# A decoder megakernel: one block end without GpSimd's drain, an earlier clearing of semaphores, and another order of the first norms of the causal attention

## The reference

```
x = x + linear_attention_and_small_experts(layernorm(x))     # layer 0
x = x + latent_cross_attention(ctx, layernorm(x))
x = x + shared_expert(n) + routed_experts(n)                 # n = layernorm(x), 8 experts, the best 2, capacity 640
x = x + causal_attention(layernorm(x))                       # layer 1, 16 heads of width 8
x = x + biased_causal_attention(layernorm(x), ctx)
x = x + best_expert(layernorm(x))
```

```
routed[token] = w0[token] * result[2 * token] + w1[token] * result[2 * token + 1]
```

## Time and profile before

| | |
|---|---|
| median of 3 runs | 1916.84 us (1915.33 to 1916.89) |
| the profiled execution's own time | 1922.22 us |
| its span, first to last instruction | 1920.4 us |
| TensorE busy | 94% of the span |
| VectorE, ScalarE, GpSimd busy | 65%, 46%, 33% |
| mean granted TensorE clock | 0.984 of full |
| routed experts end, causal attention starts | about 1260 to 1270 us into the span |

### The profile page before, as it was taken

How to read it: one execution, slowest core, us unless ns; L and a number is a source line. 1 busy time by engine, 2 the same in 40 slices (tenths; PEclk the granted TensorE clock), 3 DMA queues, 4 the chain that set the end, 5 groups by cost and what they waited for, 6 DMA issues and landing times. The chain is left out here.

```text
span 1920.4 us, 49670 instructions
## 1 busy us (share of the span) xinstructions
PE 1809.4 (94%) x19996; PEld 1346.2 (70%) x19996; DVE 1243.8 (65%) x2977; ACT 885.8 (46%) x1701; POOL 633.0 (33%) x748
## 2 busy tenths in 40 slices
PE   5899999999999999999999999978998999999978
PEld 2566666667888888888755667846766788888743
DVE  5666766646766666666643223237886888888876
ACT  1444444345555555555432213345673444545435
POOL 2111111113333333333314523333221444444547
PEclk8999999999999999999999999988999999999999
DMA  9200000000000000000010002210010000000001
GB/s 333 69 1 0 0 0 0 1 1 1 1 1 0 0 0 0 0 0 0 1 77 29 29 22 94 95 46 25 27 18 25 2 3 3 3 3 2 3 6 39
DMA packets 37909, 46.15 MB, mean 24 GB/s; under 512 B 4984, under 2 KB 32427, under 8 KB 37250
## 3 DMA queue, kind: packets, MB, share of 16 engines
q1 hardware_dynamic: 34434, 38.43, 6.3%
q0 software_dynamic: 3328, 5.58, 0.9%
HBM read 28.67 MB, written 17.10 MB: 24 GB/s over the span
## 5 line engine op out<-in xcount | busy, mean ns | idle before, releaser
L155 POOL TENSOR_TENSOR rstd<-var_eps,minus_half 128x2 f32<-128x2 f32 (+1 forms) x116 | 92.1, 794 | 477.8 <-DVE var_eps L149 477.5
L1052 POOL TENSOR_TENSOR xa_probs<-xa_probs,xa_total 128x512 f32<-128x512 f32 x128 | 133.0, 1039 | 196.4 <-DVE xa_total L1093 191.7
L1098 DVE TENSOR_REDUCE xa_top<-ps 128x4 f32<-128x512 f32 x128 | 88.1, 688 | 129.7 <-PE ps L917 128.4
L1013 ACT ACTIVATE xa_probs<-xa_probs 128x512 f32<-128x512 f32 x128 | 80.8, 631 | 157.5 <-DVE xa_probs L1101 157.5
L906 PEld LDWEIGHTS ps<-xa_kvT,pack_latent 128*128 128x128 f32 x512 | 97.8, 192 | 66.2 <-issue 43.8
L917 PE MATMUL ps<-xa_kvT,xa_qT 128*128 128x128 f32 x1024 | 135.2, 275 | 0.0
L933 PE MATMUL ps<-xa_probsT,xa_kv 128*128 128x512 f32 x256 | 133.2, 602 | 1.9 <-ACT xa_attnT L1022 1.8
L906 PE MATMUL ps<-xa_kvT,pack_latent 128*128 128x256 f32 x512 | 132.3, 384 | 1.4 <-PEq L344 1.4
L376 PE MATMUL ps<-la_h2T,pack_moe 128*128 128x512 f32 x256 | 128.3, 609 | 3.9 <-ACT la_hid L575 3.9
L389 PEld LDWEIGHTS ps<-pack_moe,la_hid 128*128 128x128 f32 x1024 | 119.9, 192 | 14.1 <-issue 12.0
L917 PEld LDWEIGHTS ps<-xa_kvT,xa_qT 128*128 128x128 f32 x1024 | 124.5, 192 | 0.1
(11 more groups left out here) (354 smaller groups left out, 4029.4 us busy)
## 6 DMA issues: line engine op xcount, KB each, us to landing
expert_weights<-experts_dram SPq DMA_DIRECT2D x8, 768.0 KB, 5.8
result_pairs<-zeros SPq DMA_DIRECT2D x1, 4096.0 KB, 29.3
ca_got<-result_pairs SPq DMA_DIRECT2D x16, 256.0 KB, 2.8
slot_rows<-zeros SPq DMA_DIRECT2D x1, 2880.0 KB, 18.0
expert_rows<-slot_rows SPq DMA_DIRECT2D x8, 360.0 KB, 3.3
pack_moe<-moe_dram SPq DMA_DIRECT2D x1, 2312.0 KB
pack_latent<-latent_dram SPq DMA_DIRECT2D x1, 2050.0 KB, 14.0
pack_latent<-biased_dram SPq DMA_DIRECT2D x1, 2048.0 KB, 7.5
```

What stands on the lines that cost most here:

```text
L155: pool.tensor_tensor(m.rstd[:, 0:tiles], m.var_eps[:, 0:tiles], m.minus_half[:, 0:tiles], ALU.pow).then_inc(sem.rstd, 1)
L1052: pool.tensor_tensor(probs[:, u % 4], probs[:, u % 4], over(total[:, u % 4], 2, KEYS), ALU.mult).then_inc(probs_ready, 1)
L1098: dve.tensor_reduce(top[:, s % 4], scores, AX.X, ALU.max).then_inc(top_ready, 1)
```

## The change

- The block of `run_experts` is opened with `no_gpsimd_drain=True`, so GpSimd issues no drain at its end.
- `reuse_semaphores` is called between latent attention and `routed_experts`, and no longer between `routed_experts` and the last stages. It clears the semaphores of the first two stages; those of the routed stages are neither cleared nor used again.
- In causal attention GpSimd waits, ahead of combine(1), combine(2) and combine(3), until normed(0), normed(1) and normed(2) are done.
- DVE's order becomes: stats(0), normed(0), stats(1), normed(1), stats(2); body 0: softmax(0, 0), normed(2), softmax(0, 1), stats(3); body 1: softmax(1, 0), normed(3), softmax(1, 1), normalise(0). From body 2 on it is the same as before.

```diff
-        with nc.Block() as block:
+        with nc.Block(no_gpsimd_drain=True) as block:
...
                 for step in range(STEPS):
+                    if 1 <= step <= SETS:
+                        pool.wait_ge(ln.normed, 2 * step)
                     combine(step)
                     root(step)
...
                     if ahead >= 2 and has(step, 2):
                         stats(later(step, 2))
+                    if ahead >= 2 and not has(step, 2):
+                        normed(later(step, 2))
                     if ahead == 0:
                         scale_mask()
                     if has(step, 2):
                         add(later(step, -2))
                     if here:
                         softmax(step, 1)
-                    if ahead >= 2 and not has(step, 2):
-                        stats(later(step, 2))
-                    if ahead >= 2:
+                    if not before:
+                        stats(later(step, 3))
+                    if ahead >= 2 and has(step, 2):
                         normed(later(step, 2))
...
                 for first in range(2):
                     stats(step_of(0, first))
                     normed(step_of(0, first))
+                stats(step_of(0, 2))
                 run_steps(dve, STEPS, body, DEPTH, LEAD)
...
             latent_attention(nc, m, latent)
+        reuse_semaphores(nc, m)
         routed_experts(nc, m)
-        reuse_semaphores(nc, m)
```

## The result

| | before | changed |
|---|---|---|
| median of 5 runs, us | 1915.33 (1913.71 to 1916.89) | 1905.16 (1904.29 to 1909.34) |
| ratio | | 0.9938, 95% interval 0.9914 to 0.9963 |
| profiled execution, us | 1922.22 | 1909.34 |
| its span, us | 1920.4 | 1907.5 |

A third of the distance to the 1909.7 is not the change's: over the five runs the median of the kernel before is itself 1.5 lower than over the three that the forecast was laid against. In a second set of runs the ratio was 0.9944 (0.9928 to 0.9961), 1908.10 against 1919.44.

What follows compares the result with a forecast made beforehand. TensorE, busy 94% of the span, was taken as the bound, its standstills as the gain. -6.0 (4.8 and 1.2) - 4.0 + 1.35 + 1.5 = -7.15 gave a median of 1909.7 us, range 1905.5 to 1914.

Steps and rivals of the forecast that it cites:

- Drain and clearing at the experts' end: Experts' end: without drain and clearing, SP's first load of got leaves at the last scatter's landing, 4.8 us earlier.
- Rival (E): Experts' end: another engine or GpSimd's sequencer stays to 1268.5 without a drain; gain 1.4, sum -3.7, 1913.1; 6%.
- the bound of 2.8: Experts' end: lower bound of the first load's gain, if the landing is final only when the drain ended, 1268.5.
- (D): Softmax delay stays, landing final only with what the drain waited for, scatters held up: +3.9, 1920.7; 4%.
- (B): Experts' end: DVE's clearing of `ca_vheads` beside the last scatters holds them up, at most 1.8; sum -5.4, 1911.4; 8%.
- Norm without GpSimd beside it: Causal start: GpSimd's wait keeps combine(1) away, normed(0) takes 0.6 to 0.7 instead of 1.88; turn_rows(0) gains 1.2.
- Order of the first steps: Causal start: softmax(1, 1) 1.7 late, then step 1 to 2 takes 10.4 instead of 16.1; balance -4.0.
- Rival (C): Causal start: DVE's 3.2 delay at stats(2) never made up, something other than normed(3) sets the 16.1; 0.0, 1916.9; 10%.
- Rival (A): Causal start: TensorE's low clock comes back, the 16.1 shrinks only by the 3.61 wait; -4.5, 1912.3; 15%.
- The clearing's new place: Before the routed stage: clearing and barrier stand in the open, +1.35, perhaps 1.1 with fewer semaphores.
- Its idle time: Before the routed stage: TensorE stands still 2.4 instead of 1.00 and loses its clock, +1.5; bounds 0 and 3.

Runs made afterwards that it cites:

- e2: Changed kernel with the semaphore clearing back between routed experts and causal attention, the drain still left out; ratio to the kernel before 0.9970.
- e5: Changed kernel without GpSimd's three added waits for normed(0), (1), (2), DVE's new order kept; ratio to the kernel before 0.9955.
- e0: The changed kernel itself, run and profiled once more; ratio to the kernel before 0.9944, median 1908.10 against 1919.44.
- e8: Changed kernel with stats(2) moved behind softmax(0, 0) instead of ahead of it; ratio to the kernel before 0.9939.
- e11: Changed kernel with DVE's order as before, except stats(3) and normed(3) ahead of softmax(1, 1); ratio to the kernel before 0.9953.
- e9: e8 with 24 transposes of a constant, into a bank nothing reads, ahead of turn_rows(0); ratio to the kernel before 0.9943.
- e1: Changed kernel with GpSimd's drain kept at the end of the routed experts' block; 0.9982, 1916.55 against 1920.09 for the kernel before.
- e3: Kernel before with only the two block-end edits, DVE's order and GpSimd's waits as before; ratio to the kernel before 0.9982.
- e6: Kernel before with both block-end edits and GpSimd's three added waits, DVE's order as before; ratio to the kernel before 0.9971.
- e7: Changed kernel with six more barriers of all engines behind the clearing, ahead of the routed stage; ratio to the kernel before 0.9976.
- e10: The kernel before, run and profiled a second time against itself; ratio 0.9999.
- e4: Changed kernel with both block-end edits undone, keeping only the new first-step order and GpSimd's waits; ratio to the kernel before 0.9988.

## Why the prediction was off, step by step

**Drain and clearing at the experts' end, -4.8: right.** The load leaves 2.32 after the last scatter's start against 7.12, exactly the landing of the earlier trace rows, in every kernel without both. Rival (E) falls with it, and so does the bound of 2.8 with the premise of (D), that the landing is final only where the drain ended: the drain's last 3.3 hang on GpSimd's instructions and not on the landing (e2). (B) did not come: the memset runs at 1259.22, beside the scatters, and these still take 0.97 and land 2.3 after their start. The Trainium skill, "SBUF — State Buffer", section "SBUF: two separate sides", would let DVE's two-port operations shut GpSimd's descriptors out; on this memset no row shows it.

**Norm without GpSimd beside it, -1.2: right in place, wrong as a term of the sum.** Normed(0) is 0.60 and turn_rows(0) 8.06 after got in the changed kernel, 9.56 before. But e5 has the 1.88 back and reaches s(3, 1) within 0.3 of e0: the added wait gives 1.2 to turn_rows(0), and by way of stats(2) takes 2.0 from softmax(0, 0) (8.84 - 6.82). It is no term of its own beside the next one.

**Order of the first steps, -4.0: right in sign, and with the term above it makes 5.8 instead of 5.2.** The delay of softmax(0, 0) came as worked out, 8.84. The 16.1 became 10.24. What I had wrong is the price of the delay: turn_rows(0) to s(1, 1) is 25.05 and 23.59 against 24.13 and 22.54 before, 1.0 late and not 1.7, and e8 shows that without stats(2) in the way it would hardly be earlier. My rate of 5.7 for the interval was one execution's; over two of each kernel it is 15.6 to 10.2, 5.4. Rival (C) is refuted by e11, whose single move turns 15.3 into 10.2. Rival (A) came half true: the low clock is back in the start (0.52 in e8, 0.50 in the changed kernel's window), and e9, with a full clock there, reaches s(3, 1) 2.2 earlier than e8. But the 16.1 did not shrink by the wait alone; it became 10.24, with the clock at 1.00.

**The clearing's new place, +1.35: 1.05.** The clear takes 0.55 and its drain 0.20 with fewer semaphores, and the gap grew from 1.00 to 2.05. The lower value that I named was the right one.

**"Its idle time", +1.5: this step failed.** I took the 0.55 behind linear attention's gap of 1.38 as what a gap of that size does, from one execution. In all nine profiled executions with the 2.05 in front of the routed stage (the changed kernel, e0, e1, e3, e5, e6, e8, e9, e11) the clock over the next 4 us was 1.00. It fell only at 4.38 (e7). And behind the 1.38 after linear attention, the same in all fourteen executions, it was 0.57 to 0.67 in seven and 1.00 in seven, so the gap alone does not settle it even there. One execution of another place was no ground for a price. 0 was the value to take, with 1.5 as the bound. The row that I read as the clock of the place itself, 968 to 969, covers only its standstill and not the matmuls behind it; their clock, over the 4 us from 969.14, was 1.00 as well.

**Not in the sum: the start of the experts, -1.6.** From the experts' first matmul to the last scatter it takes 114.0 and not 115.6. The clock over the first 5 us there is 0.66 to 0.73 in the kernel before, e10 and e4, and 1.00 in all eleven others. The three have both block ends of before; e1 and e2, with one each, have the full clock (and 114.5, as has e3, with both ends changed). The edits lie 180 us ahead of that place and 110 behind it, and TensorE stands still in front of it for 1.26 or 1.27 in all fourteen. E2 has the full clock although its clearing, too, stands where it did before. Three out of three and eleven out of eleven looks like more than chance, but the grouping was made after the fact, and behind linear attention one and the same code had both clocks. Whether the change reaches that place at all, and how, stays open.

The parts as measured are -4.8, -5.8, +1.05 and -1.6, -11.1 in all, and -9.5 without the experts' start; the two sets of runs gave 10.2 and 11.3 by their medians, which does not tell the two sums apart. With the forecast's 7.15, the missing 3 to 4 us are the clock before the routed stage (1.5), the experts' start (up to 1.6), the order (0.6) and the clearing (0.3). That the halves alone gave less by their ratios (e3, e4) stands against this account as far as their wide intervals allow; in the stretch that holds the changes their profiles add up.

Two numbers of the range were wrong in themselves. Its low end, by its own terms, adds up to 1909.7 - 1.5 - 0.25 - 2 = 1905.95 and not 1905.5. And single executions of the kernel before lay between 1913.7 and 1926.0 over all sets of runs, 0.6% apart, where I had taken 0.2% to tell two apart.

## What to carry to other kernels

A drain or clearing at a block end costs at most what lies between the moment the next stage's data is there and the barrier, so compare the drain's end with the landing of the last transfer, and with the first instruction that needs it; other short drains left in the same place take over a part of the wait. Where a pipeline's second or third step starts late, look for the one early operation that stands in an engine's queue behind work it does not need: moving that one gave all of the order's gain that could be measured here, and the moves around it gave none. Look also at the block end behind a drain that was taken out: its work can come up there, and it is free only if GpSimd is early. Before a stall is charged with the lower clock, look at the same stall in more than one execution, and at longer and shorter ones.

## What the runs showed of the hardware that I had not expected

- Two drains on GpSimd behind the same scatters end at different points: the block's (6.92, and e1) 3.33 after the last scatter's instruction, the clearing's (3.67, e2) 0.26 after it. Where the block's is left out, the next block's drain ends 3.34 after GpSimd's last instruction instead of 0.08, 190 us after the scatters landed.
- TensorE's clock kept its full level through a standstill of 2.05 in nine of nine executions, lost it at 4.38 in the one that was tried and around turn_rows(0) at 3.0 to 4.4 in seven of eight, and at one place had lost it behind 1.38 in seven of fourteen executions of the same code.
- 2.84 us of idle transposes in front of a first dependent matmul kept the clock at 1.00 where it was 0.52 and brought the first softmax 2.0 forward against e8, without a measurable gain for the whole.
